# A graph network on one core: placing the edge rows in front of layer 0 instead of during it, and summing by placed rows

## Chip, cores, metric

One core of one Trainium2 chip. The metric is device microseconds of one execution of the whole program; shown are three runs of the kernel before, and one execution under the hardware profiler.

## What is computed

12500 nodes with 128 features each, 200000 edges with a source and a destination, sorted by destination.

```python
def gnn0(h, src, dst, W1, b1, W2, b2, eps):        # 3 layers
    for l in range(3):
        agg = segment_sum(h[src], dst, num_segments=n)
        z = (1.0 + eps[l]) * h + agg
        h = maximum(z @ W1[l] + b1[l], 0.0) @ W2[l] + b2[l]
    return h

def gnn1(h, w, a, src, dst):                       # attention over edges
    e = leaky_relu(concat([h[src], h[dst]]) @ w, 0.2) @ a
    att = exp(e) / segment_sum(exp(e), src)[src]
    return segment_sum(h[src] * att, dst, num_segments=n)

x = layernorm(x + gnn0(x, ...))
x = layernorm(x + gnn1(x, ...))
```

## The kernel before

The program is written engine by engine: each engine has its own list of instructions and loops, and semaphores (`wait_ge`, `then_inc`) order them. Nodes are cut into 98 windows of 128. Edges are cut into rows of 128 (1563 rows; padded to T2 = 1568). As edges are sorted by destination, a row touches one window or two; a row with two is called a split row.

Five passes go over all rows: three layer passes, a score pass, and a last pass that sums weighted sources. Between them lie dense stages over 25 blocks of 4 windows.

**A layer pass**, `gather_rows`, `one_hots`, `sum_rows` and `layer_sums` on four engines, works like this for each row of 128 edges:
- SP (`stage`, L584) copies the source indices of 8 rows from `row_src_t` to `idx_now`, 64 rows ahead at most.
- POOL (`gather`, L797) fetches the 128 source rows of the table (512 bytes each) by an indirect DMA into a ring of 32 slots. It waits on `rows_used` for a free slot, every 4 rows, and on `staged`.
- ACT (`distances`, L953, and `hots`, L961) makes for each row a 128 x 256 table of ones and zeros: which edge goes to which node of the first or second window of the row. L953 is one call per row of 256 columns, L961 one per 4 rows of 1024.
- PE (L1198) multiplies gathered row by table, 128 x 256 sums in PSUM for each row, 4 rows (a quad) at a time, and adds 4 to `rows_used`. Four quads can be in hand.
- DVE (`add_quad`, L1618) adds the two halves of each row's sums to the `agg` windows of the row: 2 adds per row. The window numbers come from memory into registers (`load_windows`, L477), 8 at a time; a register instruction (`sums_of`, L1595) works out the address ahead of each add. Each add waits for the one before it (`added`).

All of DVE, ACT and SP work in turns of 16 rows (98 turns a pass); a turn of DVE has 32 adds and 4 loads of 8 windows.

**Two orders of the rows.** The layer passes use the given order, where any row may be a split row, so each row gets two halves. The score and last passes use a placed order: each turn of 16 rows has at most one split row, and it stands first. The numbers for this order come from 16 small dependent steps on DVE (L1567 to L1587) in set-up. While layer 0 ends, after its last gather, POOL scatters the edge rows to their places with 26 indirect DMAs (`place_rows`, L789: 13 for the sources, 13 for the positions in the window with the two window numbers). After layer 0's dense stage SP loads them back (L663, L664), PE flips them (`flip_edges(2, ...)`, `flip_edges(3, ...)`, L1240), and DVE stores them to `src_t` and `rel_t` (`placed_edges`, L1629); SP writes the placed window numbers out and, before the score pass, loads them to `tile_win`.

**Set-up.** SP loads the edges. DVE finds the windows of each row, and checks that the edges are in order (the branch for those that aren't is not taken here). `e_srcf` and `e_rel` are flipped by PE into `row_src_t` and `row_rel_t`, the first 8 stagings go out, POOL begins to gather, and beside it DVE makes the places, while PE and ACT flip and scale x into `agg` (L529, L912), which all sums of layer 0 need.

Of the kernel before, what the change touches and what calls it, by code (L numbers as in the profile page):

```python
# [9 lines left out]
f32 = mybir.dt.float32  # L10
bf16 = mybir.dt.bfloat16
i32 = mybir.dt.int32
# [60 lines left out]
RELW = P + 2  # L73
# [41 lines left out]
def gnn(nc, x, src, dst, w1, b1, w2, b2, eps, w, a, out):  # L115
    ctx = ExitStack()
    with ctx:
# [15 lines left out]
        row_info = nc.dram_tensor("row_info", (2 * RG, P), i32).ap()  # L133
# [3 lines left out]
        placed_src = nc.dram_tensor("placed_src", (QROWS, P), f32).ap()  # L137
        placed_rel = nc.dram_tensor("placed_rel", (QROWS, RELW), f32).ap()
# [33 lines left out]
        e_mid = big[:, e_at:e_at + QROWS]  # L172
        e_srcf = e_mid.rearrange("p (r e) -> p r e", r=RG)
        e_relw = big[:, e_at + QROWS:e_at + QROWS + RG * RELW].rearrange("p (r e) -> p r e", r=RG)
        e_rel = e_relw[:, :, 0:P]
        g_at = e_at + QROWS + RG * RELW
        g_srcf = per_tile(g_at)
        g_relw = big[:, g_at + QROWS:g_at + QROWS + RG * RELW].rearrange("p (r e) -> p r e", r=RG)
        g_rel = g_relw[:, :, 0:P]
        assert 2 * QROWS <= g_at and g_at + QROWS + RG * RELW <= 6 * QROWS  # L180

# [30 lines left out]
        row_wins = hot_mem[0:1, :].bitcast(i32)  # L212
# [10 lines left out]
        row_src_t = exp_rel[:, 0, 0:T2].bitcast(i32)  # L223
        row_rel_t = exp_rel[:, 1, 0:T2]
# [87 lines left out]
        info = piece(P)  # L312
        info_t = piece(P).bitcast(i32)
# [64 lines left out]
        info_ready = sem("info_ready")  # L378
# [3 lines left out]
        wins_in = sem("wins_in")  # L382
# [21 lines left out]
        added = sems("added", HALF)  # L404
# [56 lines left out]
        WEIGHTS = 10  # L461
        X_PARTS, PART = 4, -(-(CHUNKS - 1) // 4)
# [73 lines left out]
        def _(sp):  # L536
            flat = "q e -> (q e)"

# [11 lines left out]
            for given, ours in ((src, edge_src), (dst, edge_dst)):  # L550
                sp.dma_start(ours.rearrange(flat)[0:E].rearrange("(p e) -> p e", p=EP),
                             given.rearrange("(p e) -> p e", p=EP)).then_inc(edges_in, 16)
            for ours, pad in ((edge_src, pad_src), (edge_dst, pad_dst)):
                sp.dma_start(ours.rearrange(flat)[E:QPAD].rearrange("(p e) -> p e", p=PP),
                             pad).then_inc(edges_in, 16)
# [30 lines left out]
            def stage_first():  # L586

                for lane in range(AHEAD):
                    stage(row_src_t, lane, lane)
# [1335 lines left out]
```

## Time and profile before

| | |
|---|---|
| median of 3 runs | 10925.52 us (10924.64 to 10935.29) |
| the profiled execution | 10923.18 us, its span 10921.5 |
| instructions in the span | 146396 |
| busy: PE / PE's weight loads / DVE / ACT / POOL | 55% / 43% / 48% / 44% / 63% |
| mean granted clock of TensorE | 0.751 |
| layer pass 0, first gather to last add | 48.0 to 2430.3 us |
| layer pass 1 | 2479.7 to 4824.3 us |
| layer pass 2 | 4855.7 to about 7184 us |
| score pass | from about 7305 us to about 9745 |

Times are microseconds from the span's start. Busy time counts the engines' work proper; register, branch and semaphore instructions of an engine's sequencer (marked with a q, as DVEq) are not in it. "issue" as a releaser means that the profile shows nothing that the engine waited for.

### The profile page before, as it was taken

What the parts mean: (1) busy time and instruction counts of PE and PEld (TensorE: products, weight loads), DVE (VectorE), ACT (ScalarE), POOL (GpSimd) and SP (SyncE); (2) the same over time, 40 slices, a digit from 0 to 9 for tenths busy, and PEclk for the clock granted to TensorE, in tenths of its full rate; (3) what the DMA queues carried; (4) which work ended last, traced back from release to release, by engine and by line L of the source; (5) the groups of instructions that cost most, each with busy time, mean ns of one, the idle gap of its engine ahead of it and who ended that gap; (6) DMA issues with size and microseconds to landing.
All of it is one profiled execution on the core that took longest, in us unless ns stands there. A gap on an engine that the chain in (4) does not pass through costs nothing.

```text
span 10921.5 us, 146396 instructions
## 1 busy us (share of the span) xinstructions
PE 5953.6 (55%) x27350; PEld 4733.0 (43%) x27351; DVE 5274.4 (48%) x18105; ACT 4813.0 (44%) x10884; POOL 6934.4 (63%) x7404
## 2 busy tenths in 40 slices
PE   4444445445444444454444444456666666667776
PEld 3333333333332333333333333345666666666665
DVE  3333333333343344333333333355665665568888
ACT  4444444435444444454444444432222222227777
POOL 4666666655666666646666666646666666658886
PEclk7677776777777776777777777778778877779998
DMA  2111111122111111121111111135555555544444
GB/s 78 45 45 45 45 45 45 45 50 63 45 45 45 46 45 45 45 62 45 45 45 45 45 46 45 45 110 147 148 148 147 148 149 146 148 131 140 140 139 134
DMA packets 918938, 878.50 MB, mean 80 GB/s; under 512 B 253625, under 2 KB 764543, under 8 KB 918844
## 3 DMA queue, kind: packets, MB, share of 16 engines
q0 software_dynamic: 239936, 516.96, 18.6%
q1 hardware_dynamic: 615258, 261.67, 8.7%
q10 hardware_dynamic: 63698, 99.36, 3.3%
q8 instruction: 15, 0.25, 0.0%
q14 instruction: 31, 0.25, 0.0%
HBM read 736.57 MB, written 139.68 MB: 80 GB/s over the span
## 4 chain that ended last, share of the span: by engine, by line
issue 30%; DVE 25%; DVEq 22%; PE 12%; another core or an unknown queue 7%; ACT 3%; ACTq 0%; DMA 0%; SPq 0%; POOL 0%; POOLq 0%
DVE agg L1618 15%; DVEq L1595 12%; DVEq L477 6%; PE psum L1279 4%; DVE agg L1604 3%; PE psum L1198 3%; PE psum L1304 2%; PE psum L1298 2%; DVEq L1617 2%; DVE big L1853 1%; DVE work L1727 1%; DVE work L1734 1%; DVEq L1622 1%; ACT hot L1076 1%
## 5 line engine op out<-in xcount | busy, mean ns | idle before, releaser
L1198 PE MATMUL psum<-work,rows 128*128 128x256 f32 x9408 | 3258.4, 511 | 3640.5 <-DVE agg L1618 1878.4
L1618 DVE TENSOR_TENSOR agg<-agg,psum 128x128 f32 x9408 | 2704.7, 287 | 4290.7 <-issue 3430.2
L1198 PEld LDWEIGHTS psum<-work,rows 128*128 128x128 f32 x9408 | 2343.7, 260 | 4554.8 <-issue 3447.7
L797 POOL DMA_INDIRECT rows<-table_g,idx_now x3136 | 2958.6, 943 | 1782.5 <-issue 1032.0
L961 ACT ACTIVATE work<-big,one_col 128x1024 f32<-128x1024 f32 x1176 | 1334.6, 1140 | 3485.9 <-remote 2969.7
L797 POOL DMA_INDIRECT rows<-in_x,idx_now x1568 | 1479.8, 944 | 896.0 <-issue 500.3
L953 ACT ACTIVATE big<-iota_w,rel_now 128x256 f32<-128x256 f32 x4704 | 1971.8, 495 | 56.8 <-remote 5.1
L1037 ACT ACTIVATE work<-psum 128x256 f32<-128x256 f32 x784 | 294.7, 387 | 1861.5 <-remote 1109.4
L797 POOL DMA_INDIRECT rows<-table_p,idx_now x784 | 761.0, 971 | 481.2 <-SPq L625 252.3
L1279 PE MATMUL psum<-work 128*128 128x98 f32 x3168 | 621.0, 360 | 689.3 <-DVE work L1727 376.2
L1279 PEld LDWEIGHTS psum<-work 128*128 128x128 f32 x3168 | 565.8, 268 | 741.4 <-DVE work L1727 407.1
L1298 PE MATMUL psum<-big,work 128*128 x3136 | 774.1, 334 | 165.2 <-DVE work L1753 123.9
L797 POOL DMA_INDIRECT work<-table_p,idx_now x588 | 574.2, 976 | 379.5 <-SPq L625 215.5
L1340 PE MATMUL psum<-rows,hot 128*128 128x128 f32 x3328 | 659.4, 326 | 228.7 <-ACT hot L1076 176.0
L1298 PEld LDWEIGHTS psum<-big,work 128*128 128x128 f32 x3136 | 605.7, 239 | 192.2 <-issue 189.0
L1340 PEld LDWEIGHTS psum<-rows,hot 128*128 128x128 f32 x3328 | 494.9, 206 | 374.6 <-ACT hot L1076 214.3
L859 POOL TENSOR_SCALAR hot<-iota_w,big 128x128 f32<-128x128 f32 x624 | 490.4, 790 | 73.2 <-issue 64.3
L867 POOL DMA_INDIRECT big<-table_r,idx_now x416 | 411.0, 988 | 149.5 <-issue 99.3
L1604 DVE TENSOR_TENSOR agg<-agg,psum 128x128 f32 x1664 | 476.8, 287 | 53.2 <-PE psum L1340 2.4
L1724 DVE TENSOR_TENSOR work<-psum,hilo 128x392 f32<-128x392 f32 x396 | 222.4, 562 | 574.4 <-remote 427.9
L1076 ACT ACTIVATE hot<-big 128x128 f32<-128x128 f32 x1040 | 477.7, 478 | 0.0
L1734 DVE TENSOR_TENSOR work<-work,psum 128x516 f32<-128x516 f32 x392 | 269.9, 689 | 399.5 <-ACT work L1038 320.8
(218 smaller groups left out, 5545.5 us busy)
## 6 DMA issues: line engine op xcount, KB each, us to landing
rows<-x_of SPq DMA_DIRECT2D x415, 256.0 KB
rows<-table_g,idx_now POOLq DMA_INDIRECT x3136
work<-rel_rows ACTq DMA_DIRECT2D x196, 256.0 KB
x_of<-rows SPq DMA_DIRECT2D x196, 256.0 KB
big<-lo_rows ACTq DMA_DIRECT2D x208, 192.0 KB
x_of<-work SPq DMA_DIRECT2D x147, 256.0 KB
rows<-in_x,idx_now POOLq DMA_INDIRECT x1568
rows<-table_p,idx_now POOLq DMA_INDIRECT x784
```

The source lines that it names most:

```text
L477: _, values = nc.values_load_multi_w_load_instructions(of[0:1, ds(first, n)], engines=(engine,), min_val=0, max_val=WINS - 1, skip_runtime ...
L797: pool.indirect_dma_start(out=to, out_offset=None, in_=table, in_offset=bass.IndirectOffsetOnAxis(ap=idx_now[:, at:at + 1], axis=0)) \
L953: ins = act.activation(span_away[q % 2][:, j, :], iota_w[:, :], ACT.Abs, bias=rel_now[:, t:t + 1])
L961: act.activation(span_hot[q], span_away[q % 2], ACT.Relu, bias=one_col[:, :], scale=-1.0).then_inc(hot_ready, 1)
L1076: act.activation(hot[:, j, :], away[:, n % 2, :], ACT.Relu, bias=scalars[:, h, 0, 0, j:j + 1], scale=scalars[:, h, 0, 1, j:j + 1]).then_in ...
L1198: ins = pe.matmul(sums_at(q, t % QUAD), ring[:, t, :], span_hot[q][:, t % QUAD, :], start=True, stop=True)
L1279: ins = pe.matmul(den_ps, den_hot[:, t % 8, 1, :], den_hot[:, t % 8, 0, 0:HI], start=False, stop=False)
L1298: pe.matmul(sums, hot_t[:, t // QUAD, (t % QUAD) * P:(t % QUAD + 1) * P], q_rows[:, ds(windows[t - h * HALF] * PW, PW)], start=True, stop= ...
L1340: pe.matmul(ps[j // 2][:, (j % 2) * D:(j % 2 + 1) * D], hot[:, j, :], row_of(h * HALF + j, D), start=True, stop=True).then_inc(rows_used, 1)
L1595: dve.lower_ap(to)
L1604: dve.tensor_tensor(to, to, sums, ALU.add).then_inc(bank_free, 1)
L1618: dve.tensor_tensor(to, to, sums_at(q, j)[:, k * P:(k + 1) * P], ALU.add).then_inc(added[a], 1)
```

## The change

Rows are placed before layer 0, and all five passes use the placed order.

- Source and position of an edge row, and its two windows, lie side by side in one row of 258 floats, `placed`, so 13 scatters do instead of 26. They stand in front of the first gather, and wait for the 16 steps on DVE, which are moved ahead. The casting of the sources moves from DVE to POOL.
- SP loads the placed rows back before the first staging. PE flips 16 of the 25 blocks of x first, then the placed rows, then the other 9 blocks. DVE fills `src_t` and `rel_t`; `row_src_t`, `row_rel_t` and the window list by given rows are gone. The placed windows go out and back to `tile_win` before layer 0.
- In the layer passes only the first row of 16 gets 256 columns; the others get 128. DVE makes 17 adds in 16 rows instead of 32, with 3 loads of windows instead of 4 (two of 8, one of 1).
- The copies of the edge lists in HBM are made in the branch that is not taken.

```diff
+            def flip_x(b): ...
+            pe.wait_ge(nodes_in, 16 * (X_PARTS + 1))
+            for b in range(X_EARLY):
+                flip_x(b)
+            pe.wait_ge(places_ready, 1)
+            pe.wait_ge(src_in, 16)
+            flip_edges(0, g_srcf)
+            pe.wait_ge(dst_in, 16)
+            flip_edges(1, g_rel)
...
+            for b in range(X_EARLY, BLOCKS):
+                flip_x(b)
...
-            gather_rows(0, x, D)
-
             pool.wait_ge(g_ready, 2)
             pool.wait_ge(places_ready, 1)
-            place_rows(placed_src, e_srcf)
-            place_rows(placed_rel, e_relw)
+            for r in range(RG):
+                pool.indirect_dma_start(out=placed, out_offset=bass.IndirectOffsetOnAxis(ap=place_i[:, r:r + 1], axis=0),
+                                        in_=e_all[:, r, :], in_offset=None).then_inc(rows_placed, 16)
+            gather_rows(0, x, D)
...
+            sp.wait_ge(rows_placed, 16 * RG)
+            for to, c0, c1, landed in ((g_srcf, 0, P, src_in), (g_all[:, :, P:PLACED], P, PLACED, dst_in)):
+                sp.dma_start(to, placed[:, c0:c1].rearrange("(r p) e -> p r e", p=P)).then_inc(landed, 16)
             sp.wait_ge(g_taken, QUADS)
             stage_first()
...
-                        ins = act.activation(span_away[q % 2][:, j, :], iota_w[:, :], ACT.Abs, bias=rel_now[:, t:t + 1])
+                        wide = 2 * P if t == 0 else P
+                        ins = act.activation(span_away[q % 2][:, j, 0:wide], iota_w[:, 0:wide], ACT.Abs, bias=rel_now[:, t:t + 1])
...
-                    act.activation(span_hot[q], span_away[q % 2], ACT.Relu, bias=one_col[:, :], scale=-1.0).then_inc(hot_ready, 1)
+                    if q == 0:
+                        act.activation(span_hot[q][:, 0, P:2 * P], span_away[q % 2][:, 0, P:2 * P], ACT.Relu, bias=one_col[:, :], scale=-1.0)
+                    act.activation(span_hot[q][:, :, 0:P], span_away[q % 2][:, :, 0:P], ACT.Relu, bias=one_col[:, :],
+                                   scale=-1.0).then_inc(hot_ready, 1)
...
-                        ins = pe.matmul(sums_at(q, t % QUAD), ring[:, t, :], span_hot[q][:, t % QUAD, :], start=True, stop=True)
+                        wide = P if t % TPI else 2 * P
+                        ins = pe.matmul(sums_at(q, t % QUAD)[:, 0:wide], ring[:, t, :], span_hot[q][:, t % QUAD, 0:wide],
+                                        start=True, stop=True)
...
+            def add_quad(l, turn, q, windows, second):
 
                 quad = l * QUADS2 + turn * IN_HAND + q
                 for j in range(QUAD):
+                    to = sums_of(windows[(q % 2) * QUAD + j])
+                    if j == 0:
+                        dve.wait_ge(rows_used, USED + l * T2 + turn * TPI + (q + 1) * QUAD)
+                        dve.wait_ge(added[QUAD - 1], IN_HAND + quad)
+                    elif j == 1 and q == 0:
+                        dve.wait_ge(seconds_added, l * TURNS2 + turn + 1)
+                    else:
+                        dve.wait_ge(added[j - 1], IN_HAND + quad + 1)
+                    dve.tensor_tensor(to, to, sums_at(q, j)[:, 0:P], ALU.add).then_inc(added[j], 1)
+                    if j == 0 and q == 0:
+                        to = sums_of(second[0])
+                        dve.wait_ge(added[0], IN_HAND + quad + 1)
+                        dve.tensor_tensor(to, to, sums_at(q, j)[:, P:2 * P], ALU.add).then_inc(seconds_added, 1)
```

## Rows read from the trace of the kernel before

**Rows 1.** The page, busy us (share of the span) by engine

```profile
PE 5953.6 (55%) x27350; PEld 4733.0 (43%) x27351; DVE 5274.4 (48%) x18105; ACT 4813.0 (44%) x10884; POOL 6934.4 (63%) x7404
```

**Rows 2.** The page, the chain that ended last, by line

```profile
DVE agg L1618 15%; DVEq L1595 12%; DVEq L477 6%; PE psum L1279 4%; DVE agg L1604 3%; PE psum L1198 3%; PE psum L1304 2%; PE psum L1298 2%; DVEq L1617 2%; DVE big L1853 1%; DVE work L1727 1%; DVE work L1734 1%; DVEq L1622 1%; ACT hot L1076 1%
```

**Rows 3.** Busy us by stretch: pass 0, its tail, pass 1

```profile
core 0: us, PE busy (x) PEld busy (x) DVE busy (x) ACT busy (x) POOL busy (x), PEclk, DMA share, GB/s
115.00:2378.00 2263.00, 1087.51 (x3087) 780.03 (x3087) 882.43 (x3070) 1088.78 (x2029) 1448.11 (x1535) 0.71 0.18 45
2379.00:2431.00 52.00, 13.63 (x41) 9.73 (x42) 18.43 (x64) 7.15 (x12) 25.27 (x27) 0.66 0.16 36
2535.00:4793.00 2258.00, 1060.96 (x3076) 764.28 (x3076) 879.16 (x3058) 1073.69 (x2017) 1448.41 (x1536) 0.71 0.18 45
```

**Rows 4.** Groups by line, pass 0: xcount, busy us, mean ns, idle before, releasers

```profile
L797 POOL DMA_INDIRECT rows<-in_x,idx_now x1535 | 1448.1, 943 | 841.4 <-issue 445.7 <-remote 329.0 <-PE psum L1198 66.7
...
L1618 DVE TENSOR_TENSOR agg<-agg,psum 128x128 f32 x3070 | 882.7, 288 | 1437.7 <-issue 1156.5 <-PE psum L1198 84.4 <-DVE agg L1618 70.0
...
L961 ACT ACTIVATE work<-big,one_col 128x1024 f32<-128x1024 f32 x386 | 437.9, 1140 | 1143.9 <-remote 1030.1 <-PE psum L1198 66.7 <-issue 46.9
```

**Rows 5.** Timeline of POOL, pass 0: start us, us, instruction [idle before]

```profile
1006.34 0.94 POOL L797 DMA_INDIRECT rows<-in_x,idx_now  x1 [3.86 <-remote]
...
1029.96 0.94 POOL L797 DMA_INDIRECT rows<-in_x,idx_now  x1 [3.94 <-remote]
...
1048.68 0.94 POOL L797 DMA_INDIRECT rows<-in_x,idx_now  x1 [0.31 <-issue]
```

**Rows 6.** Timeline of DVE, the same stretch

```profile
1007.83 5.18 DVE L1618 TENSOR_TENSOR agg<-agg,psum 128x128 f32 x16 [1.37 <-issue]
...
1019.95 0.29 DVE L1618 TENSOR_TENSOR agg<-agg,psum 128x128 f32 x1 [1.10 <-issue]
```

**Rows 7.** Line L1595, two stretches: ns min/median/max, first and last start

```profile
L1595 DVEq FUSED_REGOPS  x16: 57/61/75, 1007.6 to 1012.4; - x16
...
L1595 DVEq FUSED_REGOPS  x11: 3/698/709, 1016.4 to 1029.0; - x11
```

**Rows 8.** Timeline, tail of pass 0; the scatter shown is the last

```profile
2398.62 0.29 DVE L1618 TENSOR_TENSOR agg<-agg,psum 128x128 f32 x1 [1.11 <-issue]
...
2411.22 0.97 POOL L789 DMA_INDIRECT placed_rel<-big,place_i  x1 [0.30 <-issue]
...
2418.84 5.18 DVE L1618 TENSOR_TENSOR agg<-agg,psum 128x128 f32 x16 [2.43 <-issue]
```

**Rows 9.** Timeline of set-up

```profile
33.26 1.03 DVE L1526 CAST big<-rows 128x1664 f32<-128x1664 int32 x1 [7.00 <-issue]
...
48.03 1.17 POOL L797 DMA_INDIRECT rows<-in_x,idx_now  x1 [44.85 <-issue]
...
51.74 0.16 DVE L1567 COPY work<-psum 128x1 f32<-128x1 f32 x1 [2.38 <-issue]
...
57.69 0.17 DVE L1587 CAST place_i<-work 128x13 int32<-128x13 f32 x1
...
92.57 2.58 ACT L912 ACTIVATE agg<-psum,eps 128x512 f32<-128x512 f32 x4 [5.61 <-remote]
...
115.81 0.94 POOL L797 DMA_INDIRECT rows<-in_x,idx_now  x1 [27.57 <-PE psum L1198]
```

**Rows 10.** Groups by line of the last pass

```profile
L1604 DVE TENSOR_TENSOR agg<-agg,psum 128x128 f32 x1664 | 476.8, 287 | 53.2 <-PE psum L1340 2.4 <-issue 0.5
...
L1068 ACT ACTIVATE big<-iota_w,big 128x128 f32<-128x128 f32 x1040 | 394.6, 398 | 24.9 <-DVE big L1864 1.0
```

**Rows 11.** DMA issues between passes 0 and 1: KB, median us to landing

```profile
big<-placed_src SPq DMA_DIRECT2D x1, 832.0 KB, 5.6
```

**Rows 12.** Timeline, the 33rd gathers of passes 1 and 2, last adds of pass 1

```profile
2535.33 0.94 POOL L797 DMA_INDIRECT rows<-table_g,idx_now  x1 [15.88 <-PE psum L1198]
...
4819.76 4.54 DVE L1618 TENSOR_TENSOR agg<-agg,psum 128x128 f32 x14
...
4901.53 0.94 POOL L797 DMA_INDIRECT rows<-table_g,idx_now  x1 [6.17 <-remote]
```

More of the change, by code:

```diff
@@ L588, in stage_first @@
                 for lane in range(AHEAD):
[L589 removed]
+                    stage(src_t, lane, lane)
             def stage_ahead(no):
[L593 removed]
                 def used(lap, lane):
@@ L1163, in _, with flip_x @@
             pe.matmul(ps[1][:, 0:1], ones, splits[:, RG:RG + 1], start=True, stop=True).then_inc(splits_ranked, 1)
-            pe.wait_ge(nodes_in, 16 * (X_PARTS + 1))
-            for b in range(BLOCKS):
+            def flip_x(b):
                 if b >= len(X_BANKS):
@@ L1168, in _ @@
                 flip(pe, ps[X_BANKS[b % len(X_BANKS)]], lambda c: agg_chunk(b * C + c), n_chunks(b)).then_inc(x_flipped, 1)
+            pe.wait_ge(nodes_in, 16 * (X_PARTS + 1))
[6 more added lines that the diff above has]
+            flip_edges(1, g_rel)
+            for k in range(2):
+                ins = pe.transpose(ps[4][0:RG, k * P:(k + 1) * P], g_all[:, :, 2 * P + k], ident[:, :])
+            ins.then_inc(info_flipped, 1)
+            for b in range(X_EARLY, BLOCKS):
+                flip_x(b)
             pe.wait_ge(agg_scaled, BLOCKS)
@@ L1362, in _ @@
             dve.sem_inc(bank_free, HALF)
-            for j in range(HALF):
+            for j in range(QUAD):
                 dve.sem_inc(added[j], IN_HAND)
@@ L1587, in _ @@
             dve.tensor_copy(place_i[:, :], place_f).then_inc(places_ready, 1)
+            take_edges(0, src_t, QROWS)
+            take_edges(1, rel_t, QROWS)
+            dve.wait_ge(info_flipped, 1)
+            dve.tensor_copy(tile_info_t, ps[4][0:RG, 0:2 * P]).then_inc(info_taken, 1)
+            for h in range(2):
+                own.add(dve.tensor_tensor_reduce(out=junk, in0=w_pq[:, h * PW:h * PW + D], in1=a_row, scale=NEG_SLOPE, scalar=0.0,
+                                                 op0=ALU.mult, op1=ALU.add, accum_out=w_pq[:, h * PW + D:(h + 1) * PW]))
+                own.wait()
+            dve.tensor_scalar(a_08[:, 0:D], a_row, 1.0 - NEG_SLOPE, None, ALU.mult)
+            dve.memset(a_08[:, D:PW], 1.0)
+            dve.wait_ge(weights_in, 16 * WEIGHTS)
+            for l in range(LAYERS - 1):
+                ins = dve.tensor_scalar(b2_wide[:, l, :], ones[:, :], b2_col[:, l:l + 1], None, ALU.mult)
+            ins.then_inc(b2_ready, 1)
             dve.wait_ge(agg_scaled, BLOCKS)
-            dve.wait_ge(wins_in, 16)
+            dve.wait_ge(info_in, 32)
             def sums_of(window):
```

184 lines of the change are left out of this document (53 added, 131 removed).

## The prediction

> **What bounds it now.** I read the page first, for shares: no engine is busy above 63% [rows 1], so something waits. The chain of waits says where: a third of it is the adds at L1618 and the register work ahead of them (L1595, L477), all on DVE [rows 2]. The stages then show that the three layer passes take 2251 to 2263 us each (two of them in rows 3), 6.8 of the 10.9 ms; the change edits these, and the score and last passes keep their code.
>
> In one pass [rows 4] DVE is busy 883 of 2263 us and idle for 1157 that nothing in the profile ends ("issue"); ACT waits 1030 for others; POOL works 1448 in 1535 gathers of 943 ns. POOL's timeline has the rhythm [rows 5]: 16 gathers in a row, one per 1.248 us (1029.96 to 1048.68 are 15 steps), then a gap of 3.9. Gathers alone would take 1535 x 1.248 = 1916 us; the other 347 are 96 gaps, each 3.62 beyond the normal 0.30. POOL stops when its ring of 32 rows is full, and that is because DVE is late.
>
> DVE is not late by arithmetic. The add takes 0.29 us at all times, but in one stretch adds follow at 0.32 us (16 in 5.18), in another at 1.4 [rows 6]; the register instruction ahead of each takes 61 ns in the first and 698 in the second [rows 7]. The second, seen from 1016.4 to 1029.0, begins some 10 us after POOL resumed (1006.3) and ends 3 us after POOL stopped (1026.0); POOL resumes 0.9 later. The tail of the pass shows it again: 1.4 us an add while scatters run back to back until 2412.2, and 4.5 us after them 16 in 5.18 us again [rows 8]. In set-up, with DVE idle, 32 gathers in a row hold up the handoffs of PE and ACT, until 4.4 us after they end (88.2 to 92.6) [rows 9]. So I take it that back-to-back gathers for over 10 us make each sequencer instruction of DVE cost 0.70 us, and that a 3 us pause cures it. No row shows what they share.
>
> **The layer pass after.** Per 16 rows DVE issues 32 adds with a register instruction each (64), 4 window loads with one each (8), 4 waits, and 2 for the loop: 78. After it is 17 x 2 + 3 x 2 + 4 + 2 = 46.
> - Slow: 46 x 0.70 / 16 = 2.0 us a row (now 3.4). POOL brings one per 1.248, so the backlog still grows, by 0.80 - 0.50 = 0.30 rows per us.
> - Fast: 17 x 0.32 = 5.4, 3 loads of about 0.7 each (the 1.37 us gap ahead of the 16 adds holds two [rows 6]) 2.1, waits 0.4: 8.0 us for 16 rows, 0.50 a row. ACT is near it. No row shows its distances at 128 columns in this loop; the nearest, in the last pass, is 395 / 1040 = 0.38 us [rows 10], and half of L961's 1.14 [rows 4] is 0.57, with a fixed part perhaps 0.65. 4 x 0.38 + 0.65 + 0.1 = 2.3 per 4 rows, 0.57 a row. PE's products at half width take less than its 4 x 2 x 0.52 of busy time now. I take 0.57; the bounds are 0.50 and today's fast pace of 0.85 (32 x 0.32 + 4 x 0.7 + 0.4 = 13.5 for 16).
> - A cycle: fast for some 10.9 us (0.9 before POOL resumes, 10 after). 10.9 / 0.57 = 19 rows used, 8 gathered: the ring empties by 11, and the pause's 3 slow us free 1.5 more. To refill 12.5 rows at 0.30 takes 41 us. POOL runs 51 us, 41 rows, between pauses, where it now runs 16.
> - 1535 / 41 = 37 pauses of 3.62 = 134 us; with 1916 that is 2050 a pass, 1.335 us a row. Against 2263, 2258 and 2251: **-622**.
>
> Bounds: at 0.85 a row the ring empties by 6 and refills in 20 us, 24 rows a run: 64 pauses, 2148 a pass, -328. No pauses: 1916 a pass, **-1024**; DVE is then 40% busy, POOL alone sets the pace, and no edit of DVE gets below that. A gain below nothing in this term is rival 3.
>
> **The second product**, on 1 tile of 16, adds an ACT call of 128 columns, an add and a register load a turn, all counted above. What PE and ACT save in columns lies beside POOL's gathers and counts for nothing by itself.
>
> **Set-up.** Now the first gather goes at 48.0, the ring is full at 88.2, and POOL idles until 115.8 for the first sums, which need x flipped and scaled [rows 9]. After, ahead of the first gather: DVE resumes at 33.3 and makes three passes of 1.9 over the edges and small ones: 40. The dependent steps take 6.1 (51.7 to 57.9 now): 46. 13 scatters at 1.27 [rows 8]: 63; landing 2: 65. The first of two loads back, 5.6 [rows 11]: 71. Flips and casts 4: 75. The first of SP's 8 stagings lands in 2 to 3, POOL's start 1 more: first gather near 79, ring full at 119. PE has flipped 16 of 25 blocks by then; the other 9, at 0.7 to 0.9 each (4 of ACT's calls took 2.58 [rows 9]), end near 88, before the gathers' run is 10 us old. About 8 handoffs follow, which may wait 3 us each: first sums at 100 to 123. So the 33rd gather goes at 119 to 123: **+6**. Bounds +3, and +31 if today's 67.8 us between first and 33rd gather return (79 + 67.8). SP also waits for the flipped windows and makes three small transfers before its next staging, which is due 32 rows later; DVE's new wait for them ends near 92. The dropped copies of the edge lists were on no one's path: zero.
>
> **Ends of the passes.** Pass 0 has 52 us from last gather to last add, 33 of them 26 scatters that keep DVE slow [rows 3, 8]. They are gone; a landing, 3 slow us and a backlog of some 15 rows at 0.57 are left, about 20: **-32**. Pass 1 takes 31 (4793 to 4824), pass 2 the same; at 20 each: **-22** [rows 12]. Pass 1 lets POOL idle 15.9 us on a full ring, pass 2 only 6.2 [rows 12]; the difference is PE's 28 flips of placed rows, which go: **-10**. The conversions that stay run on DVE while POOL fills the ring.
>
> **Sum.** -622 + 6 - 32 - 22 - 10 = -680. The profiled execution took 10923.2 (span 10921.5), 2.3 under the median of the runs shown, nothing here. I predict **10240**, this case alone 10120 to 10400.
>
> **The rivals.**
> 1. *The hold-up of DVE goes away or stops mattering*: 10923 - 1024 - 70 = 9830. For: in the last pass the same add has 53 us of idle time in 1664 [rows 10], so register work as such is cheap; demand falls from 78 instructions in 23.6 us to 46 in 20. Against: 0.70 us each allows 1.43 a us, and 46 / 19.97 is 2.3; set-up shows the hold-up with DVE idle. 0.25.
>  A page's rule lands there too. The Trainium skill ("Runtime: NRT & Kernel Launch", Instruction fetch mechanics) says that a taken branch to a target outside the fetched pages stalls the engine. By that rule the slow stretch belongs to the loop's back edge. As a mechanism of this kernel: 10 us of stall a turn and 8 of work are 18, under POOL's 19.97, so 9830 again. The rows speak against it: the tail's slow stretch ends with the scatters, and 16 adds later in the same loop are fast.
> 2. *The ring empties little*: drain at today's pace, or dearer slow instructions; a pause every 20 to 24 rows, 2148 a pass: 10923 - 328 - 45 = 10550. For: 0.57 rests on rows of another pass. 0.12.
> 3. *Slower: pauses no longer cure.* POOL's gap could shrink below the 3 us that the cure takes, and it would go on in runs of 4 with the hold-up standing. At 2.0 us a row a pass takes 3070: 10923 + 3 x 813 = 13360. It decides once less than a seventh of the time is fast (now 10.9 of 23.6 us): 0.14/0.57 + 0.86/2.0 = 0.68 rows a us, today's pace. Against: POOL's gap ends just as the hold-up does, as if it waited for the cure itself. 0.04.
> 4. *Nothing comes of it*: a latency beside DVE sets the 23.6 us (ACT and PE idle half the pass). 0.02.
>
> My case has 0.57. The range takes rival 1 whole and stops short of 2 to 4: 9800 to 10520. No change is what lies within 0.2% (22 us), about what a measurement of this kernel can tell: 0.02; faster 0.94; slower 0.04.
>
> **What would show it.** Right: POOL's runs grow from 16 to 30 to 60 gathers, gaps stay near 3.9 us, register instructions of 0.70 us remain, a pass takes 2000 to 2100. Rival 1: no gaps, ACT and DVE wait for rows. Rival 2: runs of 20 to 24. Rival 3: runs of 4. Set-up: first gather near 79, 33rd near 121. Wrong altogether if the score or last pass moves.

## The result, and the profile after

The changed kernel takes 10758.89 us (median of 4 runs, 10756.46 to 10763.38); the kernel before took 10925.08 beside it (4 runs, 10924.63 to 10935.29). The ratio is 0.9846, with a 95% interval of 0.9834 to 0.9857: faster by 166 us. I had forecast 680, so the sign is right and the time lies outside my range. The profiled execution took 10763.38 us (span 10761.6), 160 less than that of before. Times that are compared come from executions at full pace; one of e2's four took 13019 us at a granted clock of 0.38, where its others had 0.75, and is left out.

The page after, busy us by engine, answers to [rows 1]:

```profile
PE 4749.1 (44%) x27323; PEld 4216.7 (39%) x27324; DVE 3994.5 (37%) x13681; ACT 3909.3 (36%) x11178; POOL 6943.5 (65%) x7392
```

The work did shrink as the diff says: DVE's instructions fell by 4424, and its busy time by 1280 us. No engine was the bound, before or after, and the time hardly followed.

Busy us by stretch, after: pass 0 and pass 1, each from its 33rd to its last gather, as in [rows 3]:

```profile
core 0: us, PE busy (x) PEld busy (x) DVE busy (x) ACT busy (x) POOL busy (x), PEclk, DMA share, GB/s
118.00:2346.00 2228.00, 665.54 (x3087) 589.49 (x3086) 467.29 (x1627) 792.00 (x2121) 1452.08 (x1536) 0.59 0.18 46
...
2458.00:4680.00 2222.00, 673.55 (x3088) 597.74 (x3086) 468.46 (x1631) 780.99 (x2122) 1452.13 (x1536) 0.58 0.18 46
```

DVE is busy 467 us of a pass, not 882, and the pass is shorter by 35. From the starts of the 33rd and the last gather of each pass in both traces, the 160 us split so:

| stretch | before | after | difference |
|---|---|---|---|
| start to the 33rd gather | 115.8 | 117.9 | +2 |
| pass 0, 33rd to last gather | 2262.3 | 2227.7 | -35 |
| to the 33rd gather of pass 1 | 157.2 | 112.6 | -45 |
| pass 1 | 2257.4 | 2221.4 | -36 |
| to the 33rd of pass 2 | 108.8 | 92.3 | -16 |
| pass 2 | 2250.9 | 2228.5 | -22 |
| to the 33rd of the score pass | 193.8 | 172.6 | -21 |
| score pass | 2398.8 | 2400.9 | +2 |
| rest | 1176.5 | 1187.7 | +11 |

The three passes give 93, where I had 622. The ends and starts give 80, where I had 58.

Groups by line in pass 0, after; they answer to [rows 4]:

```profile
L766 POOL DMA_INDIRECT rows<-in_x,idx_now x1536 | 1452.8, 946 | 776.2 <-issue 458.1 <-remote 316.6 <-PE psum L1178 1.5
...
L1585 DVE TENSOR_TENSOR agg<-agg,psum 128x128 f32 x1532 | 440.0, 287 | 1731.0 <-remote 1068.3 <-issue 564.5 <-DVE agg L1585 28.9
L933 ACT ACTIVATE work<-big,one_col 128x512 f32<-128x512 f32 x384 | 267.3, 710 | 1093.2 <-remote 982.8 <-PE psum L1178 55.2 <-issue 55.2
```

What was DVE's own idle time ("issue", 1157 us in [rows 4]) is now largely time in which it waits for a count from elsewhere ("remote", 1068). ACT waits as long as before. POOL, which I wanted to free, still idles 776 us.

A stretch of pass 0 shows whose count that is. In POOL's timeline a run of 24 gathers ends, and the gap behind it is longer than those in [rows 5] (3.9):

```profile
517.66 0.95 POOL L766 DMA_INDIRECT rows<-in_x,idx_now  x1 [0.30 <-issue]
523.82 0.95 POOL L766 DMA_INDIRECT rows<-in_x,idx_now  x1 [5.21 <-remote]
```

The next run ends at 553.5. Timelines of PE, ACT and DVE near its end:

```profile
544.29 2.04 PE L1178 MATMUL psum<-work,rows 128*128 128x128 f32 x8 [7.05 <-issue]
558.55 2.04 PE L1178 MATMUL psum<-work,rows 128*128 128x128 f32 x8 [12.22 <-DVE agg L1585]
...
537.45 0.72 ACT L933 ACTIVATE work<-big,one_col 128x512 f32<-128x512 f32 x1 [3.99 <-issue]
557.06 0.72 ACT L933 ACTIVATE work<-big,one_col 128x512 f32<-128x512 f32 x1 [18.89 <-remote]
...
543.76 0.29 DVE L1585 TENSOR_TENSOR agg<-agg,psum 128x128 f32 x1 [1.11 <-issue]
557.06 0.93 DVE L1585 TENSOR_TENSOR agg<-agg,psum 128x128 f32 x3 [13.01 <-remote]
```

PE ends its products at 546.3. ACT and DVE both wait for `rows_used`, PE's count of them, and both go on in the same instant, 557.06: 10.7 us later, and 3.5 us after POOL stopped. DVE has nothing to add in between. Its 0.70 us register instructions are there as before (at 540.2 and 543.0, for instance), but the ring fills for a count that is late whatever DVE does. So in this stretch my reason for the full ring was not the reason.

### The profile page after: what moved, and what is told of

The parts are those of the page before. It is cut to its first block, busy times and chain, and to the rows that moved or that the text cites. A ratio compares the mean times of both kernels' runs of the same rounds, so it can differ in the third digit from the quotient of the medians.

```text
span 10761.6 us, 137184 instructions
## 1 busy us (share of the span) xinstructions
PE 4749.1 (44%) x27323; PEld 4216.7 (39%) x27324; DVE 3994.5 (37%) x13681; ACT 3909.3 (36%) x11178; POOL 6943.5 (65%) x7392
## 4 chain that ended last, share of the span: by engine, by line
issue 26%; another core or an unknown queue 23%; DVE 20%; DVEq 17%; PE 11%; ACT 2%; DMA 0%; ACTq 0%; POOL 0%; SPq 0%; POOLq 0%
DVE agg L1585 8%; DVEq L1562 7%; DVEq L468 5%; DVE agg L1571 4%; PE psum L1251 4%; PE psum L1276 2%; DVEq L1580 2%; PE psum L1270 2%; DVE big L1818 2%; DVEq L1593 1%; DVE work L1692 1%; DVE work L1699 1%; PE psum L1178 1%; DVE work L1689 1%
## 5 line engine op out<-in xcount | busy, mean ns | idle before, releaser
L1178 PE MATMUL psum<-work,rows 128*128 128x128 f32 (+1 forms) x9408 | 2056.2, 394 | 4728.1 <-DVE agg L1585 2465.2
L1178 PEld LDWEIGHTS psum<-work,rows 128*128 128x128 f32 x9408 | 1825.5, 284 | 4959.6 <-issue 2822.9
L1585 DVE TENSOR_TENSOR agg<-agg,psum 128x128 f32 x4704 | 1351.4, 287 | 5323.6 <-remote 3145.3
L933 ACT ACTIVATE work<-big,one_col 128x512 f32<-128x512 f32 x1176 | 817.9, 710 | 3315.9 <-remote 2837.2
L923 ACT ACTIVATE big<-iota_w,rel_now 128x128 f32<-128x128 f32 (+1 forms) x4704 | 1501.6, 396 | 429.5 <-remote 345.0
L1571 DVE TENSOR_TENSOR agg<-agg,psum 128x128 f32 x1664 | 476.8, 287 | 51.8 <-PE psum L1312 1.2
```

The costliest lines, as they stand in the source:

```text
L923: ins = act.activation(span_away[q % 2][:, j, 0:wide], iota_w[:, 0:wide], ACT.Abs, bias=rel_now[:, t:t + 1])
L933: act.activation(span_hot[q][:, :, 0:P], span_away[q % 2][:, :, 0:P], ACT.Relu, bias=one_col[:, :], scale=-1.0).then_inc(hot_ready, 1)
L1178: ins = pe.matmul(sums_at(q, t % QUAD)[:, 0:wide], ring[:, t, :], span_hot[q][:, t % QUAD, 0:wide], start=True, stop=True)
L1571: dve.tensor_tensor(to, to, sums, ALU.add).then_inc(bank_free, 1)
L1585: dve.tensor_tensor(to, to, sums_at(q, j)[:, 0:P], ALU.add).then_inc(added[j], 1)
```

## The experiments

All are edits of the changed kernel, and are shown shortened, some lines in simpler words than the code's. In the expectations R is the recorded theory (DVE's slow instructions fill the ring), L is that PE's count of used rows is late whatever DVE does, and S is that something behind POOL sets the rate of gathers. A pass is measured from its 33rd gather to its last. e1, e2, e5 and e9 ran four times, the others once.

### Fewer and more adds

```
-                for j in range(QUAD):
+                for j in (0, QUAD - 1):          # e1: two of four main adds left out
...
-                        wide = P if t % TPI else 2 * P
+                        wide = 2 * P              # e2: ACT and PE at 256 columns again,
+                                                  # and DVE adds the second half for every tile
```

> The changed kernel with the second and third main add of every four tiles left out (with their register work), so the sums are incomplete; PE and ACT do all they did. DVE issues 9 adds a turn of 16 rows, not 17: 30 instructions, not 46. Theory R (the recorded one: register instructions of 0.70 us, times their number, fill the ring): a slow row costs 30 x 0.70 / 16 = 1.31 us against POOL's 1.248, the ring fills hardly ever, a pass comes near 1920 to 1980 us instead of 2228, the whole near 9900. Theory L (formed on the trace after: PE's count of used rows reaches POOL, ACT and DVE 9 to 15 us late while gathers follow one another, whatever DVE does): the pass moves by less than 60 us, the whole is 10600 to 10760.

> One part undone: the rows keep the new order and the early scatter, but every one-hot is 256 columns wide again and DVE makes 32 adds a turn, the second of each pair with zeros. What is left of the gain is that of the order and the set-up, tails and starts. R and L both allow the passes to go back to 2251 to 2263 us (3 x 31 = 93 us more than after): 10850. If it stays at 10759, the 17 sums gave nothing and the passes' 31 us came from elsewhere; if it goes above 10925, placing first alone costs.

e1: 10734.69 us, ratio to before 0.9824 (0.9808 to 0.9841), 24 us under the change; its passes take 2219.6, 2216.4 and 2218.3. e2: 10829.20 us, 0.9913 (0.9893 to 0.9932), 70 above the change; its passes take 2232.8, 2231.0 and 2234.8, where I had expected 2251 to 2263.

e2 says where the gain came from. Its tables, products and adds are as wide and as many as before the change, and still it keeps 72 of the 93 us that the change takes off the passes; the 15 adds fewer in 16 rows and the narrower tables gave the other 21. What e2 keeps is the placed order and shorter register work: the traces have 68 DVE instructions of all kinds in a turn of 16 rows for e2, 78 before the change, 46 after it. No run separates the order from the count of instructions. Between the passes e2 keeps 49 us, and the narrower work gives 33 more.

Pass 0 of e1, groups by line:

```profile
L1585 DVE TENSOR_TENSOR agg<-agg,psum 128x128 f32 x772 | 221.9, 287 | 2011.6 <-remote 1443.4 <-issue 429.1 <-PE psum L1178 104.5
```

The engine idles 2012 us ahead of these adds, in a window of 2228, and the pass is 8 us shorter. Of DVE's register instructions in pass 1, 448 of 2013 took 0.6 to 0.8 us in the changed kernel and 31 of 1245 in e1, while the pass went from 2221 to 2216. R falls: its slow instructions nearly vanish and almost nothing comes of it. 30, 46 and 68 DVE instructions a turn (e1, the change, e2) give passes of 2218, 2226 and 2233.

### A pause, a shorter ring

e5 waits after each 16th gather until it has landed:

```
+                if no != LAYER_A and lane % 2 == 1:
+                    pool.wait_ge(row_in[(lane * HALF + HALF - 1) % RING // 2],
+                                 pairs(no, lap * (LAP // RING) + lane * HALF // RING))
```

> In the layer passes POOL waits after every 16th gather until it has landed, a pause of about 2.2 us instead of 0.30 between two gathers. L and R, if so short a pause clears the hold-up: 96 pauses of 1.9 us, 1916 + 182 = 2098 a pass, the whole near 10370. If it takes the 3 us or more that the gaps on a full ring last, the late counts stay, the ring fills as it does now and the pauses come on top of that or take the place of some: 2228 to 2410 a pass, 10760 to 11300.

10751.91 us, 0.9843 (0.9826 to 0.9859): no different from the change. The expectation had 10370 if so short a pause cures and 10760 or more if not; it doesn't cure. Idle stretches of POOL between 1 and 3 us add up to 110 to 207 us more in a pass than in the change, and those above 3 us to 106 to 197 less; passes take 2226.9, 2218.6 and 2222.2. Pauses that are put in replace others.

e8 lets POOL run ahead by 16, 8 and 24 rows in the three passes:

```
-pool.wait_ge(rows_used, USED - RING + no * T2 + ...)
+pool.wait_ge(rows_used, USED - {0: 16, 1: 8, 2: 24}[no] + no * T2 + ...)
```

> The changed kernel with fewer rows of the ring in use in the layer passes: 16 (pass 0), 8 (pass 1), 24 (pass 2), not 32. S: the mean rate is set behind POOL, so the passes of 16 and 24 stay within 40 us of 2220, with shorter runs and shorter gaps; 8 rows hold 10 us of gathers against a landing of 2.2 us and the handoffs, 2250 to 2500. L: runs of 16 stop before the hold-up is long: shorter late counts but 96 gaps of 3 us and more, 2250 or more; runs of 8 never see it (it begins 10 us into a run): 192 gaps of 1 to 2 us, 2200 to 2300.

10788.37 us; windows over the three passes:

```profile
126.00:2349.00 2223.00, 967.39 (x3064) 734.25 (x3064) 471.97 (x1645) 785.81 (x2103) 1450.94 (x1536) 0.50 0.18 46
2466.00:4723.00 2257.00, 968.90 (x3069) 735.28 (x3068) 467.57 (x1628) 787.33 (x2091) 1450.78 (x1535) 0.50 0.18 45
4808.00:7030.00 2222.00, 829.38 (x3076) 686.10 (x3076) 468.92 (x1632) 776.95 (x2112) 1451.31 (x1536) 0.53 0.18 46
```

Half the ring changes nothing. With a quarter of it the pass takes 2257, and no register instruction of DVE is slow: min, median and max in ns over pass 1 are

```profile
L1562 DVEq FUSED_REGOPS  x1517: 65/69/75, 2500.2 to 4594.9; - x190
```

PE's counts are late there all the same. A quad's last products end at 3010.53, and DVE adds them 5.3 us later:

```profile
3009.31 1.22 PE L1178 MATMUL psum<-work,rows 128*128 128x128 f32 x4 [1.18 <-DMA rows<-table_g,idx_now]
...
3015.81 1.25 DVE L1585 TENSOR_TENSOR agg<-agg,psum 128x128 f32 x4 [9.04 <-PE psum L1178]
```

DVE's slow instructions are gone here, with a pause of POOL every 16 gathers, and the pass is as long as before the change. So they are not needed for a pass of that length. How much of the 2257 is due to having 8 rows ahead only isn't separated.

### What a gather costs

e6 puts POOL work between gathers, e7 makes the gathers smaller, e15 leaves out every second one of pass 0.

```
+                    for w in {0: (128,), 1: (128, 128), 2: (1,)}[no]:    # e6, each behind a wait for the last
+                        pool.memset(hot_second[:, 0:w], 0.0)
...
+                n, cols = {0: (P // 2, D), 1: (P, D // 2), 2: (P // 4, D), 3: (P, ROW)}[no]    # e7
...
-                    gather(lane, j, table, wide)
+                    if not (no == 0 and j % 2 == 1):                     # e15
+                        gather(lane, j, table, wide)
```

> The changed kernel, with POOL work between gathers in the layer passes: behind each gather a memset of 128 columns (pass 0), two of them (pass 1), or one of 1 column (pass 2), so that POOL's pitch goes from 1.25 to some 1.5, 1.75 and 1.4 us without pauses. Theory S (new after the first four runs, where 30, 46 and 76 DVE instructions a turn and a pause every 16 gathers all gave passes of 2216 to 2235 us): what lies behind POOL takes some 1.443 us a gather, POOL runs ahead of it, and what the other engines send waits behind; so passes take max(1.443, pitch) x 1535: pass 0 some 2300 without gaps on a full ring and with PE's counts prompt, pass 1 some 2690, pass 2 near 2220 with fewer gaps. Theory L (long runs of gathers hold up PE's counts, and only a pause of POOL cures): the gaps come on top, pass 0 takes 2500 or more and the counts stay late.

> The changed kernel with smaller gathers in the layer passes, so that sums are of wrong or stale rows: 64 rows of 512 bytes (pass 0), 128 rows of 256 bytes (pass 1), 32 rows of 512 bytes (pass 2). S by count of rows: the path takes 1.443 us for 128 rows, about 0.72 and 0.36 for 64 and 32; passes 0 and 2 have no hold-up and run at POOL's pitch (1.25 or less a gather: 1919 us or less), pass 1 stays at 2220. S by bytes: pass 1 too falls to 1919. L, with the number of gathers in a row as the cause: all three stay near 2220.

> The changed kernel with every second gather of pass 0 left out (PE uses the row beside it in its place), so that pass 0's sums are wrong; 784 gathers, and all products, adds and counts as ever. Passes 1 and 2 as they were. Theory S, as the run without users now has it: the path behind POOL takes 1.39 us a gather (2131 us for 1535, with nobody using rows and POOL never stopped by a full ring) and a little for the other engines' instructions; so pass 0 takes half of 1.39 x 1535 and the whole of that little (2224 - 2131 = 93): 1065 + 93 = 1160 us. If POOL's pitch of 1.25 us were the floor and the rest had to do with used rows, it takes 960 + 305 = 1265. If the hold-up is gone with half the gathers, 960 to 980.

e7 took 10742.50 us. Windows over its three passes (64 rows; 128 rows of 256 bytes; 32 rows), the last two figures DMA share and GB/s:

```profile
125.00:2348.00 2223.00, 710.08 (x3111) 628.23 (x3110) 471.88 (x1643) 797.84 (x2137) 1384.34 (x1535) 0.57 0.10 23
2456.00:4677.00 2221.00, 688.74 (x3088) 616.05 (x3088) 471.31 (x1640) 782.31 (x2124) 1451.25 (x1536) 0.58 0.13 23
4768.00:6982.00 2214.00, 701.98 (x3104) 624.81 (x3103) 470.81 (x1639) 786.13 (x2133) 1327.50 (x1536) 0.57 0.06 12
```

A quarter of the rows and of the bytes, and the pass is 15 us shorter than the change's (2213.4 for 2228.5). Both forms of S in the expectation, by rows and by bytes, fail. What costs is the gather as an instruction.

e6 (11826.99 us) was a coarser tool than I thought: the second memset's wait brought the pitch, the time from one gather's start to the next, to 2.1 us, not 1.75. Passes took 2265, 3223 and 2238. In pass 1, at 2.1 us a gather, counts are prompt: PE's products begun at 3003.08 for 1.22 us are followed by DVE's add at

```profile
3004.44 0.29 DVE L1592 TENSOR_TENSOR agg<-agg,psum 128x128 f32 x1 [9.76 <-PE psum L1185]
```

0.14 us after they end, and none of DVE's 2016 register instructions takes over 0.1 us. Pass 0, at a pitch of 1.33, kept late counts (products that ended at 1014.4 let ACT and DVE go on at 1023.7, both at once) and its gaps, against S, and took 1.476 us a gather; only 41 of DVE's 2011 register instructions took 0.6 to 0.8 us. So a pitch of 1.33 leaves the late counts, and one of 2.1 doesn't. No run lies between.

e15 (9784.35 us, on a chip where the kernel before took 11048.02, 1% more than elsewhere): pass 0 takes 1146.8 us from its 33rd gather to its last, 1504 rows with 752 gathers, where my expectation scaled to these rows is 1137 (pass 1, with all its gathers, took 2245 there). Halving the gathers took almost half away, though DVE, ACT and PE did all their work.

### Nobody uses the rows

e12 leaves work out by pass:

```
+                        if no == 0:                    # PE: no products, a count from its queue
+                            if t % QUAD == QUAD - 1:
+                                pe.sem_inc(rows_used, QUAD)
+                            continue
...
-            one_hots(0)                                # ACT and DVE: nothing in passes 0 and 1
-            one_hots(1)
```

> The changed kernel with work left out, so that its sums are wrong. Pass 0: PE makes no products and only counts the rows from its queue as they land, ACT and DVE do nothing. Pass 1: PE makes its products (with constant one-hots) and counts them as ever, ACT and DVE do nothing. Pass 2 as it was. Theory S: the rate is set behind POOL, whoever uses the rows, 2220 in all three. Theory P (the counts of PE's products are what is late, and nothing else sets the pass): pass 0 runs without gaps at 1.25 us a gather, 1920 us; pass 1 stays at 2215 to 2225. Theory C (ACT's and DVE's work makes the counts late): both at 1920.

10632.32 us; windows over the three passes, and POOL's group in the first:

```profile
118.00:2249.00 2131.00, 0.00 (x0) 0.00 (x0) 0.00 (x0) 0.00 (x0) 1588.25 (x1535) 0.50 0.18 48
2368.00:4558.00 2190.00, 882.52 (x3089) 692.05 (x3088) 0.00 (x0) 4.32 (x9) 1451.61 (x1536) 0.55 0.17 46
4635.00:6860.00 2225.00, 676.82 (x3072) 602.77 (x3072) 467.96 (x1630) 777.43 (x2112) 1452.14 (x1536) 0.58 0.17 46
```

```profile
L766 POOL DMA_INDIRECT rows<-in_x,idx_now x1535 | 1588.7, 1035 | 542.8 <-issue 542.5 <-PEq L1184 0.3
```

This is the run that settles the floor; none of the three expectations had it. In pass 0 PE, ACT and DVE do no work, and POOL never waits for the ring (its idle time is "issue"). Still it takes 2131 us, 1.388 a gather. Its timeline shows how: 158 gathers come at the pitch of 1.25 that I took for the floor, then some are stretched; from the 200th on the mean pitch is 1.40.

```profile
120.03 0.94 POOL L766 DMA_INDIRECT rows<-in_x,idx_now  x1 [0.30 <-issue]
121.27 0.95 POOL L766 DMA_INDIRECT rows<-in_x,idx_now  x1 [0.30 <-issue]
...
1078.02 1.57 POOL L766 DMA_INDIRECT rows<-in_x,idx_now  x1 [0.30 <-issue]
1079.89 1.10 POOL L766 DMA_INDIRECT rows<-in_x,idx_now  x1 [0.30 <-issue]
1081.30 1.09 POOL L766 DMA_INDIRECT rows<-in_x,idx_now  x1 [0.30 <-issue]
```

It looks as if POOL hands on gathers faster than something behind it takes them, and pays when that is full. But it isn't the transfers that pile up. Over the window 76:276, which holds the first 159 gathers, the DMA view has

```profile
q0 software_dynamic: 5054, 10.36, 18.9%
rows<-in_x,idx_now POOLq DMA_INDIRECT x159
```

and a gather has 32 packets on this queue (16 of data, 16 of counts), so 158 of the 159 had been carried out when the stretching began. By the packets of all of pass 0, half of the gathers have landed 2.2 us after POOL began them, 99% within 3.0 and all within 4.3. What is full, if something is, no run shows.

With PE's products the pass takes 2190, with everyone 2225: the rest of the engines together cost 93 us, of which the change could take a part. e15 and the pass of e12 agree. In e15, 16 rows take 23.4 us with 16 gathers (pass 1) and 12.2 with 8 (pass 0), so a gather costs 1.40 and all else 1.0 us per 16 rows; in e12 it is 1.39 and 93 / 96 = 0.97.

### Without gathers, and with plain transfers

e3 leaves out pass 0's gathers; e16 makes them plain transfers from POOL's queue, same size, and adds empty DVE instructions in passes 1 and 2.

```
+                if no == 0:                            # e16
+                    pool.dma_start(to, table[(at % RING) * P:(at % RING + 1) * P, :]).then_inc(landed, 16)
+                    return
...
+                    for _ in range({0: 0, 1: 2, 2: 8}[l]):
+                        dve.nop()
```

> The changed kernel with pass 0's gathers left out: POOL only raises the count that PE waits for, and the ring holds zeros. The other passes gather as they did. L and R: with no gathers there is neither hold-up; register instructions take 61 ns, PE's counts land within 1 us, and the pass goes at the pace of ACT and DVE, 8.0 to 9.1 us a turn of 16 rows, 98 turns in 780 to 900 us instead of 2228. Rival F (instruction fetch at the loops' back edges stalls DVE or PE): slow stretches stay, the pass takes 1500 us or more.

> The changed kernel with two edits. Pass 0's gathers are plain transfers from POOL's queue of 128 neighbouring rows each (same bytes, no index list; sums of wrong rows). If the 1.39 us belong to each transfer that POOL writes the lists for, pass 0 stays near 2220; if they belong to indexed gathers only, or POOL writes a plain one more slowly, the pass follows POOL's new pitch. Pass 1 has 2 more empty instructions on DVE ahead of each main add (32 a turn), pass 2 has 8 (128 a turn). Theory S with a little for each other instruction (before to after, 32 DVE instructions a turn fewer gave 31 to 35 us a pass, some 10 ns each; 16 fewer again gave 4 to 10 us, some 4 ns each): pass 1 +12 to +31 us over 2225, pass 2 +50 to +125. The recorded theory, 0.70 us for each DVE instruction in the hold-up: pass 1 some 2400 and pass 2 above 5000.

e3 took 9306.05 us; its pass 0 has 784 us from 125, some 34 us after its first product, to the last product at 909. e16 took 9306.38 us. Its pass 0:

```profile
96.00:904.00 808.00, 536.32 (x3094) 476.47 (x3093) 472.27 (x1646) 777.77 (x2123) 806.92 (x1536) 0.85 0.44 126
```

```profile
L767 POOL DMA_DIRECT2D rows<-in_x x1536 | 807.3, 535 | 1.2 <-issue 1.2
L1181 PE MATMUL psum<-work,rows 128*128 128x128 f32 (+1 forms) x3094 | 536.6, 336 | 270.6 <-ACT work L936 269.9
```

The same bytes and as many landings, 2.75 times as fast (126 GB/s, not 46), no gap, ACT busy 96% of the time and everybody served at once. So it is not bytes, not landings and not PE's counts as such. It isn't the back edges of the loops either, rival F of e3: the loops are the same, and no register instruction of DVE takes over 0.1 us in either pass. The rule that a taken branch to a target outside the fetched pages stalls the engine (the Trainium skill, "Runtime: NRT & Kernel Launch", Instruction fetch mechanics) would have left its slow stretches in both runs, and neither shows one. What is left is the indexed gather. The empty instructions left no rows in the trace, and passes 1 and 2 took 2221 and 2222, so that half tells nothing; e17 repeats it.

### Counts and their ways

Three runs on what travels beside the gathers: PE counts after each product (e9), SP stages in two transfers (e11), PE waits for its own count and passes it on (e14).

```
-                        if t % QUAD == QUAD - 1:
-                            ins.then_inc(rows_used, QUAD)
+                        ins.then_inc(rows_used, 1)                            # e9
...
+                for k in range(2):                                            # e11: 4 columns each
+                    sp.dma_start(idx_now[:, ...QUAD...], of[:, ...QUAD...]).then_inc(staged[lane], 16)
...
+                            ins.then_inc(pe_own, 1)                           # e14
+                            pe.wait_ge(pe_own, quads so far)
+                            pe.sem_inc(rows_used, QUAD)
```

> The changed kernel with PE counting a used row after each product, not four after every fourth: four times as many counts on their way to POOL, ACT, DVE and SP. S and L: counts wait behind gathers, their number matters little: passes within 20 us of 2225, the whole 10740 to 10800. If each count costs about what a DVE register instruction does in the hold-up (0.7 us), 12 more a turn would add several hundred us.

> The changed kernel with SP's staging of 8 index columns made in two transfers of 4, so that each pass has 196 more small transfers (and their 16 counts each) beside its 1568 gathers. Theory S (a path behind POOL that takes some 1.443 us for each gather, of whatever size: gathers of 128, 64 and 32 rows gave passes of 2220, 2223 and 2213 us): if that path serves the counts of any transfer, 196 more cost up to 283 us a pass, passes near 2500; if it serves POOL's alone, passes stay within 15 us of 2225, the whole 10740 to 10800.

> The changed kernel with a relay on PE in the layer passes: the fourth product of four counts for PE alone, PE waits for it and then raises the count of used rows from its queue. P, if only the way from a product's end to other engines is slow: PE sees its own count at once, the others get the queue's count at once, passes fall to 1920 to 1950 us, the whole to 9850. P, if a product's count is late for everybody: PE now stands still as long as the others did, and since it can't go on with the next four rows, passes are longer than 2225, by up to several hundred us. S: 2220, as POOL's path sets it.

e9: 10763.17 us, 0.9850 (0.9834 to 0.9867). e11: 10783.41, passes 2229.6, 2225.8 and 2227.3. In neither does a pass move by more than 5 us. e14: 10838.10, passes 2250.2, 2247.8 and 2253.2, that is 22 to 26 more each. PE's products now wait 1276 us of pass 0 for PE's own count:

```profile
PE psum L1179 <- remote: 1276.3, 172, 17.5
```

(The view of waits: us in all, times, longest.) S had passes of 2220. So a product's count is late for everybody, PE too, and not on the way to one engine.

### More work for DVE

```
+                    for _ in range({0: 0, 1: 1, 2: 3}[l]):
+                        dve.sem_inc(pad_done, 1)
```

> The changed kernel with more semaphore instructions on DVE ahead of each main add, on a semaphore nobody waits for: one in pass 1 (16 a turn), three in pass 2 (48 a turn), none in pass 0. Theory S with some 10 ns for each other instruction: pass 0 2225, pass 1 +16 us, pass 2 +48 us, the whole 10800 to 10840. The recorded theory (0.70 us for each DVE instruction while gathers follow one another, and the ring fills for it): 62 instructions a turn in pass 1 give a slow row 2.7 us, 94 in pass 2 give 4.1, passes of some 2240 and above 2400, the whole above 10950.

11018.24 us, on a chip where the kernel before took 11011.06, so passes are compared within this run; windows over them:

```profile
117.00:2357.00 2240.00, 699.69 (x3099) 621.63 (x3098) 471.00 (x1639) 795.62 (x2133) 1448.31 (x1537) 0.58 0.17 45
2465.00:4717.00 2252.00, 729.06 (x3088) 649.15 (x3087) 469.26 (x1633) 785.91 (x2130) 1448.09 (x1536) 0.56 0.17 45
4806.00:7210.00 2404.00, 758.22 (x3052) 662.85 (x3053) 466.55 (x1620) 801.37 (x2114) 1448.38 (x1537) 0.55 0.16 42
```

With 62 DVE instructions a turn (60 of them have rows in the trace) the pass is 12 us longer than with 46, 8 ns for each, about as expected; with 94 it is 164 longer, 35 ns for each, where S had 48 us and R had "above 2400". This fits R's mechanism: POOL's runs shrink to 12 and 16 gathers, with slow stretches of DVE under them. So I read it that both hold and the later one sets the pass: with 30 to 68 instructions a turn the gathers do, at 2216 to 2235, and somewhere above 68 DVE's held-up instructions take over. The kernel before, with 78 and passes of 2251 to 2262, then stood near the place where the one gives way to the other, and the change had some 30 us a pass to win there. That e2 keeps most of the gain with 68 fits; its placed order is not ruled out as the reason.

## Why the prediction was wrong, point by point

**The failed step** is the floor under the passes: "Gathers alone would take 1535 x 1.248 = 1916 us; the other 347 are 96 gaps". I read the pitch inside a run of 16 and took it for what POOL can keep up. Kept up, a gather costs 1.40 us with all else idle (e12; 1.388 over the pass), 1.43 beside PE and 1.45 beside PE, ACT and DVE. The floor is 2131, and in use 2216 to 2229. Of the 347 us of gaps that I set out to remove, 2131 - 1916 = 215 are there with nobody to wait for (e12), and 2218 - 1916 = 302 with only 30 DVE instructions a turn (e1). With 2225 for a pass instead of 2050 my sum would have been -97 for the passes and -58 for set-up, ends and starts: -155, where -160 was measured between the profiled executions. That it comes so near is partly luck, for the 2225 is itself measured, and the ends and starts gave 22 us more than I had while the score and last pass took 13 more.

**The cycle built on it** (fast 10.9 us, refill at 0.30 rows a us, runs of 41) was thus without ground. Runs did grow, from 16 to mostly 24 and 28, where I had put 30 to 60 for right; but gaps grew with them, from 3.9 to as much as 5.2 behind 24 gathers and some 5.6 behind 28, so that the rate hardly changed. I had held the gap's length fixed at 3.62 because one kind of run showed one kind of gap; a gap in proportion to the run would have been a rate.

**DVE's 0.70 us** were measured right, and they seem to set the pass at 94 instructions a turn (e17, pass 2), but at 46 they don't (e1, e8). That a 3 us pause cures them was read too boldly: the tail's 16 fast adds, which I put 4.5 us behind the scatters, start 6.7 us behind them (2412.2 to 2418.84 [rows 8]). I named DVE as the cause because it was slow when the ring filled. ACT, PE and DVE were all held up at once, as set-up had shown ("32 gathers in a row hold up the handoffs of PE and ACT"), and I priced only DVE's.

**The fast pace**, 0.57 us a row within 0.50 to 0.85: e16's pass 0 takes 808 us for 1536 rows, 0.53, and e3's is like it. Right, but it does not set these passes.

**Set-up**: first gather at 77.6, forecast 79; the 33rd at 117.9, forecast 119 to 123; +2 for +6. Timeline of POOL, beside [rows 9]:

```profile
77.56 1.22 POOL L766 DMA_INDIRECT rows<-in_x,idx_now  x1 [13.66 <-DMA idx_now<-src_t]
```

**Ends and starts**: -58 forecast, -80 measured. Pass 0's last gather is at 2345.6 and its last add ends at 2363.1, 17.5 us later where I had 20. Adds after the last gather run at the fast pace, as in [rows 8]:

```profile
2352.88 2.61 DVE L1585 TENSOR_TENSOR agg<-agg,psum 128x128 f32 x8 [0.65 <-DVE agg L1585]
```

Here the forecast held: no gather follows, and DVE is fast within 3 us. The start of pass 1 came nearly as forecast: POOL waits 5.6 us for its 33rd gather, where it waited 15.9 [rows 12].

**Score and last pass**: the score pass is unchanged (2398.8 and 2400.9). The last pass, whose code is the same, is 11 us longer: 200 adds of its loop take 130.9 us, not 129.4. The prediction called it wrong altogether if that pass moved. The part of the program behind the score pass is longer by 12 to 23 us in e1, e2, e5 and e9 too, so it is no chance of one execution; its cause is open.

**The rivals.** Rival 1 (no hold-up, 9830) took the same false floor, and its 70 for the ends has no working. Rival 2 had the sign right, runs of 20 to 24, and the reason wrong, with a pass of 2148 (10550 in all). Rival 4, "a latency beside DVE sets the 23.6 us", which I gave 0.02, was nearest in time and is in kind what happened: it spoke of ACT and PE idling half the pass, and that was the sign. Its form, no change at all, was too strong.

**What stays open.** Why an indexed gather costs 1.40 us whatever its size, and a plain transfer of the same bytes 0.53 or less. A backlog behind POOL is a picture and no more. Transfers don't queue up (e12's packets), in the change's passes no gather is stretched as in e12 (99% take 0.95 us or less) and the time goes into gaps instead, and a count is 10.7 us late where a run of 24 gathers at 1.40 - 1.25 = 0.15 us each would leave only 3.6 us behind. That the floor of e12, the gaps and the late counts come from one cause is argued from equal rates (e1, e7, e8, e15) and from gaps and late counts going together (e3 and e16 have neither; e6 at 2.1 us has prompt counts and 41 gaps, where pass 0 of the change has 88), not shown further.

No version of these with right sums is faster than the change by more than its uncertainty. What the runs point to is fewer indexed gathers, since with 784 fewer the last gather of pass 0 came at 1280.6, not 2345.6 (e15, which leaves the sums wrong); how the same sums could be had with fewer wasn't tried.

## What to carry to other kernels

A pitch read inside a burst is not a rate. Before a gap is called waste, see whether it grows with the burst ahead of it, and price the floor by a run in which the producer goes on with nobody to wait for. When several engines are released in one instant, look for what is late for all of them; the engine with the most visible stall may be a fellow sufferer, and halving its work (here 8 us in 2228) is the cheap test.

## What the runs showed of the hardware, unexpected

- An indexed gather from POOL costs 1.40 us when many follow one another with the other engines idle, though POOL issues 158 of them at 1.25 first (e12). In use, its size makes next to no difference: passes of 2221 to 2229 us with 128 rows of 512 bytes, 2223 with 64 rows, 2213 with 32, 2220 with 256 bytes a row (e7). A plain transfer of 64 KB from the same queue takes 0.53 us a piece, 1536 in a row (e16).
- The transfers of such gathers don't pile up: the median gather has landed 2.2 us after POOL began it, with all of e12's pass 0 within 4.3.
- While indexed gathers come at 1.25 us each, counts that PE attaches to its products reach ACT and DVE up to 10.7 us late in the rows shown, PE itself waits for its own (up to 17.5 us, e14), and a part of DVE's register instructions take 0.70 us in place of 0.065. At a pitch of 1.33 the late counts stay (9.3 us) and few of DVE's instructions are slow; with 8 rows ahead none is slow and counts are still 5.3 us late; at 2.1 us a gather, or with plain transfers, neither is seen.
- Semaphore instructions added on DVE cost a pass 8 ns each from 46 to 62 instructions a turn, and 35 ns each on the average from 46 to 94 (e17).
